# Turning the gate weights by transposing transfers in place of TensorE, and the b2 product two slots later

## What is computed

```python
def attention(ctx, x, Wq):                       # causal, 64 tokens a sequence
    q = x @ Wq.T; k = v = ctx @ Wq.T
    return softmax(mask(q @ k.T / sqrt(128))) @ v

def ffn(x, gate_W, W1, b1, W2, b2):
    gates = softmax(x @ gate_W)                  # 8 experts
    cw = the two largest gates of a token, normed to 1, zero elsewhere
    out = x
    for e in range(8):
        h = relu(x @ W1[e] + b1[e])              # 128 -> 256
        out = out + cw[:, e:e+1] * (h @ W2[e] + b2[e])
    return out

x = x + attention(ctx, layernorm(x), Wq)
x = x + ffn(layernorm(x), gate_W, W1, b1, W2, b2)
```

## Time and profile before

| | |
|---|---|
| time, median of 3 runs | 131.17 us (130.90 to 131.28) |
| the profiled execution, its time | 130.83 us |
| the profiled execution, its span | 129.0 us |
| TensorE busy in the span | 120.3 us (93%), 1175 products |
| VectorE busy | 107.6 us (83%) |
| ScalarE busy | 93.5 us (73%) |
| GpSimd busy | 53.5 us (41%) |
| granted TensorE clock | full in all 40 slices |

### The profile page before, as it was taken

How to read it: one execution, slowest core, us unless ns; L and a number is a source line. 1 busy time by engine, 2 the same in 40 slices (tenths; PEclk the granted TensorE clock), 3 DMA queues, 4 the chain that set the end, 5 groups by cost and what they waited for, 6 DMA issues and landing times. The chain is left out here.

```text
span 129.0 us, 3295 instructions
## 1 busy us (share of the span) xinstructions
PE 120.3 (93%) x1175; PEld 90.7 (70%) x1175; DVE 107.6 (83%) x419; ACT 93.5 (73%) x191; POOL 53.5 (41%) x57
## 2 busy tenths in 40 slices
PE   6987788999979999999999999999999979999991
PEld 2585566777847768778768778778776757776690
DVE  0629998989999999989898999958998798866683
ACT  3337485999776955996779927993799467989830
POOL 7199155330094951330095640330468303345400
PEclk9999999999999999999999999999999999999999
DMA  3999900000000000200000000200000002000002
GB/s 92 321 283 321 289 26 8 0 0 0 5 0 0 0 5 3 81 0 5 0 0 5 0 3 13 68 5 0 3 0 8 0 0 86 3 0 0 5 0 81
DMA packets 9904, 5.54 MB, mean 43 GB/s; under 512 B 504, under 2 KB 9888, under 8 KB 9888
## 3 DMA queue, kind: packets, MB, share of 16 engines
q1 hardware_dynamic: 9744, 5.27, 15.2%
q10 hardware_dynamic: 144, 0.07, 0.2%
HBM read 4.28 MB, written 1.05 MB: 41 GB/s over the span
## 5 line engine op out<-in xcount | busy, mean ns | idle before, releaser
L690 POOL TENSOR_TENSOR h_lo<-h,h_hi 128x512 f16<-128x512 f32 x24 | 28.7, 1196 | 40.2 <-ACT h L571 39.9
L571 ACT ACTIVATE h<-psH,b1T 128x512 f32<-128x512 f32 x64 | 43.3, 689 | 1.1 <-PE psH L508 0.9
L570 ACT ACTIVATE h_hi<-psH,b1T 128x512 f16<-128x512 f32 x48 | 33.0, 688 | 11.5 <-PE psH L387 11.4
L864 DVE SCALAR_TENSOR_TENSOR acc<-psY,weight_y,acc 128x128 f32<-128x128 f32 x125 | 35.1, 342 | 1.4 <-PE psY L408 1.2
L383 PE MATMUL psH<-x_hi,w_hi 128*128 128x512 f16 x62 | 23.5, 379 | 1.0 <-ACT h L571 1.0
L387 PE MATMUL psH<-x_lo,w_hi 128*128 128x512 f16 x62 | 23.5, 379 | 0.0
L384 PE MATMUL psH<-x_hi,w_lo 128*128 128x512 f16 x62 | 23.5, 379 | 0.0
L848 DVE TENSOR_TENSOR h_lo<-h,h_hi 128x512 f16<-128x512 f32 x24 | 16.5, 689 | 7.8 <-ACT h L571 7.3
L408 PE MATMUL psY<-w_hi,h_hi 128*128 128x128 f16 x192 | 22.7, 219 | 0.0
L408 PE MATMUL psY<-w_lo,h_hi 128*128 128x128 f16 x192 | 22.7, 219 | 0.0
L408 PEld LDWEIGHTS psY<-w_hi,h_hi 128*128 128x128 f16 x192 | 15.3, 98 | 2.2
(11 more groups left out here) (191 smaller groups left out, 191.4 us busy)
## 6 DMA issues: line engine op xcount, KB each, us to landing
w_sb<-in_L_ffn_W_dram SPq DMA_DIRECT2D x8, 256.0 KB, 4.9
out_dram<-acc SPq DMA_DIRECT2D x3, 256.0 KB, 2.3
x_sb<-in_x_dram SPq DMA_DIRECT2D x2, 256.0 KB, 4.0
ctx_sb<-in_ctx_dram SPq DMA_DIRECT2D x2, 256.0 KB, 4.4
x_sb<-in_x_dram SPq DMA_DIRECT2D x1, 512.0 KB, 7.6
ctx_sb<-in_ctx_dram SPq DMA_DIRECT2D x1, 512.0 KB, 8.5
out_dram<-acc SPq DMA_DIRECT2D x2, 128.0 KB, 1.8
wq_sb<-in_L_xattn_Wq_dram ACTq DMA_DIRECT2D x1, 64.0 KB, 2.8
```

What stands on the lines that cost most here:

```text
L570: nc.scalar.activation(h_hi[:, C * (e % 2) + c, :], psH[c][:, :], ACT.Relu, bias=bias, scale=scale)
L571: nc.scalar.activation(h[:, C * (e % 2) + c, :], psH[c][:, :], ACT.Relu, bias=bias, scale=scale).then_inc(h_ready, 1)
L690: nc.gpsimd.tensor_tensor(h_lo[:, i, :], h[:, i, :], h_hi[:, i, :], ALU.subtract).then_inc(hlo0_ready, 1)
L864: last = nc.vector.scalar_tensor_tensor(out=o, in0=y, scalar=weight_y[:, g % 2, t, e:e + 1], in1=o, op0=ALU.mult, op1=ALU.add)
```

## The change

weight_cat becomes 128 columns a tile wide and weight_catT 128 partitions high. The 16-bit identity, its memset and its select on GpSimd go. TensorE's transposes at slot 3 and ScalarE's copy go. SP issues, for each group, four transposing transfers from SBUF to SBUF (`turn_cat`), one a tile, as soon as cat_ready and, from group 1 on, the b2 product of the group before allow it. The b2 product goes from slot 4 to slot 6 and waits for the four transfers; the addition on VectorE goes from slot 5 to slot 7. VectorE waits for the transfers of the group before ahead of writing weight_cat.

```diff
-        ident16 = sb("ident16", [P, P], fp16)
...
-        weight_cat = sb("weight_cat", [P, TG, NB2], fp16)
-        weight_catT = sb("weight_catT", [NB2, TG, P], fp16)
+        weight_cat = sb("weight_cat", [P, TG, P], fp16)
+        weight_catT = sb("weight_catT", [P, TG, P], fp16)
...
-        CAT_T, B2_PRODUCT, B2_ADD = 3, 4, 5
+        B2_PRODUCT, B2_ADD = 6, 7
...
+            def turn_cat(g):
+                sp.wait_ge(cat_ready, g + 1)
+                if g > 0:
+                    sp.wait_ge(b2_ps, g)
+                for t in range(TG):
+                    sp.dma_start_transpose(weight_catT[:, t, :], weight_cat[:, t, :]).then_inc(cat_turned, 16)
+
+            turn_cat(0)
             for g in range(0, GROUPS - 1):
+                turn_cat(g + 1)
                 store(g)
...
-            def cat_transposes(g):
-                pe.wait_ge(cat_ready, g + 1)
+            def b2_product(g):
+                pe.wait_ge(cat_turned, (g + 1) * TG * 16)
                 for t in range(TG):
-                    last = nc.tensor.transpose(cat_ps[:, t, :], weight_cat[:, t, :], ident16[:, :])
-                last.then_inc(catT_ps, 1)
-
-            def b2_product(g):
-                pe.wait_ge(catT_ready, g + 1)
-                for t in range(TG):
-                    last = nc.tensor.matmul(tiles(psD)[:, t, :], weight_catT[:, t, :], b2_cat[:, :],
+                    last = nc.tensor.matmul(tiles(psD)[:, t, :], weight_catT[0:NB2, t, :], b2_cat[:, :],
                                             start=True, stop=True)
                 last.then_inc(b2_ps, 1)
...
-            group_steps = {CAT_T: cat_transposes, B2_PRODUCT: b2_product}
...
-                if slot in group_steps:
-                    group_steps[slot](g)
+                if slot == B2_PRODUCT:
+                    b2_product(g)
...
-            def cat_out(g):
-                act.wait_ge(catT_ps, g + 1)
-                copy(weight_catT[:, :, :], cat_ps, catT_ready)
...
-                if slot == CAT_T:
-                    cat_out(g)
...
-            nc.gpsimd.memset(ident16[:, :], 0.0).then_inc(const_zero, 1)
...
-            nc.gpsimd.affine_select(out=ident16[:, :], in_=ident16[:, :], compare_op=ALU.not_equal, fill=1.0,
-                                    base=0, pattern=[[-1, P]], channel_multiplier=1).then_inc(const_zero, 1)
...
                 if a >= 1:
-                    dve.wait_ge(catT_ps, a)
+                    dve.wait_ge(cat_turned, a * TG * 16)
```

More of the change, by code:

```diff
@@ L206, in xattn_moe @@
         logits_ps, below_ready, gate_exp_ready = sem("logits_ps"), sem("below_ready"), sem("gate_exp_ready")
-        cat_ready, catT_ps, catT_ready, b2_ps, b2_added = (
-            sem("cat_ready"), sem("catT_ps"), sem("catT_ready"), sem("b2_ps"), sem("b2_added"))
+        cat_ready, cat_turned, b2_ps, b2_added = sem("cat_ready"), sem("cat_turned"), sem("b2_ps"), sem("b2_added")
         z_ps, h_ready, hlo0_ready, hlo_ready = sem("z_ps"), sem("h_ready"), sem("hlo0_ready"), sem("hlo_ready")
@@ L357, in logit_product @@
                 last.then_inc(logits_ps, 1)
-            cat_ps = psD[0:NB2, 0:TG * P // 2].bitcast(fp16).rearrange("p (t n) -> p t n", n=P)
-            def cat_transposes(g):
-                pe.wait_ge(cat_ready, g + 1)
+            def b2_product(g):
+                pe.wait_ge(cat_turned, (g + 1) * TG * 16)
                 for t in range(TG):
-                    last = nc.tensor.transpose(cat_ps[:, t, :], weight_cat[:, t, :], ident16[:, :])
-                last.then_inc(catT_ps, 1)
-            def b2_product(g):
-                pe.wait_ge(catT_ready, g + 1)
-                for t in range(TG):
-                    last = nc.tensor.matmul(tiles(psD)[:, t, :], weight_catT[:, t, :], b2_cat[:, :],
+                    last = nc.tensor.matmul(tiles(psD)[:, t, :], weight_catT[0:NB2, t, :], b2_cat[:, :],
                                             start=True, stop=True)
@@ L648, in _ @@
             nc.gpsimd.memset(ident[:, :], 0.0).then_inc(const_zero, 1)
-            nc.gpsimd.memset(ident16[:, :], 0.0).then_inc(const_zero, 1)
             nc.gpsimd.memset(mask[:, :], 0.0).then_inc(const_zero, 1)
-            pool.wait_ge(const_zero, 3)
+            pool.wait_ge(const_zero, 2)
             nc.gpsimd.affine_select(out=ident[:, :], in_=ident[:, :], compare_op=ALU.not_equal, fill=1.0, base=0,
                                     pattern=[[-1, P]], channel_multiplier=1).then_inc(const_ready, 1)
-            nc.gpsimd.affine_select(out=ident16[:, :], in_=ident16[:, :], compare_op=ALU.not_equal, fill=1.0,
-                                    base=0, pattern=[[-1, P]], channel_multiplier=1).then_inc(const_zero, 1)
             nc.gpsimd.affine_select(out=mask[:, :], in_=mask[:, :], compare_op=ALU.is_ge, fill=MASKED, base=0,
                                     pattern=[[-1, P]], channel_multiplier=1).then_inc(const_zero, 1)
+            pool.wait_ge(const_zero, 3)
+            nc.gpsimd.memset(mask[SEQ:P, 0:SEQ], MASKED).then_inc(const_zero, 1)
+            pool.wait_ge(const_zero, 4)
+            nc.gpsimd.memset(restart[:, :, :], 1.0).then_inc(const_zero, 1)
             pool.wait_ge(const_zero, 5)
[L660 to L663, removed]
             nc.gpsimd.memset(restart[:, :, 0:1], 0.0)
```

## The result

| | kernel before | changed kernel |
|---|---|---|
| median | 131.03 us (130.89 to 131.28, 4 runs) | 134.51 us (133.95 to 135.15, 4 runs) |
| ratio, 95% interval | | 1.0258 [1.0211, 1.0306] |
| profiled execution | 130.83 us, span 129.0 | 134.98 us, span 133.2 |

The change costs 2.6%, about 3.5 us. The time lies inside the stated range (130.3 to 138), but it is not the forecast of 131.2: the range reached so far only because of rival 2, and rival 2 came. Beside it VectorE made TensorE wait in group 0, as forecast, but by another mechanism and for longer.

What follows compares the result with a forecast made beforehand. TensorE was taken as the bound. Group 0's +0.75 us and groups 1 to 3's -0.69 gave +0.06 on the profiled 130.83, so 130.9; with the median 0.34 higher, 131.2 us, range 130.3 to 138.

Steps and rivals of the forecast that it cites:

- rival 2: At TensorE's b2 product: transfers outlast their window, from 0.95 us an issue; 133.0 us at 1.2, up to 160; chance 0.41.
- TensorE is the bound, and its waits for other engines decide: Between 20 and 125 us TensorE is busy 102.8 of 105.0 us; removed work shortens the run except ahead of its waits.
- 0.23 us of transposes per group: Four TensorE transposes at slot 3 go, 0.92 us over four groups; groups 1 to 3 keep 0.23 us each.
- TensorE's other waits lie elsewhere: ScalarE's four dropped copies, 2.4 us, were costed at nothing because TensorE's remaining waits for ScalarE were not there.
- Transfers at 0.6 to 0.9 us an issue: On SP's queue a group's four transfers take 4.2 to 5.4 us, hidden in windows of 5.6 to 6.6 us.
- Group 0: The moved addition makes VectorE about 0.75 us late; TensorE's gate product waits for x_lo, +0.75 us against before.
- The power should have been passed over: In group 0 GpSimd's power gets in only at 36.7, ends at 37.7, and TensorE goes on at about 39.0.
- rival 1: In group 0 the power gets in between w_lo and h_lo, VectorE loses 0.2 us at most: 130.7 us; chance 0.26.
- The other groups on VectorE: In groups 1 to 3 VectorE has idle time behind ScalarE, so the moved addition of 0.72 us fits in.
- SP, the stores, ScalarE's copies, GpSimd's start: Stores queued behind transfers, four dropped copies and GpSimd's changed start were all costed at nothing.
- The sum: For the run, +0.75 us in group 0 and -0.69 in groups 1 to 3 make +0.06 us, forecast 131.2 us.
- its case: The forecast's likeliest case, transfers hidden and group 0 late on VectorE: 130.9 to 131.6 us, chance 0.33.

Runs made afterwards that it cites:

- no_turn_45: Changed kernel with transfers and turning left out, b2 product on unturned weights, product and addition at slots 4 and 5: 131.06 us, ratio 0.9981.
- packed_pe: Kernel before with a group's weights packed into one 128 x 128 block, one TensorE transpose and a 128-column copy per group: 131.89 us, ratio 1.0012.
- idle_turns: Kernel before plus sixteen transposing transfers between two spare buffers, for which no engine waits until the last store: 131.74 us, ratio 1.0006.
- move_only: Kernel before, TensorE transposes kept, with the b2 product moved to slot 6 and its addition to slot 7: 132.94 us, ratio 1.0111.
- add_only: Kernel before with only the b2 addition moved, from slot 5 to slot 7: 132.32 us, ratio 1.0065.
- turn_later: Changed kernel with the b2 product at slot 8 and its addition at slot 9: 132.72 us, ratio 1.0105.
- turn_6_10: Changed kernel with the b2 product kept at slot 6, addition at slot 10, gate product also waiting for the addition: 133.49 us, ratio 1.0117.

## Where the prediction was right, and where it was wrong

- **TensorE is the bound, and its waits for other engines decide**: right. All of the loss behind the head is waits of TensorE.
- **0.23 us of transposes per group**: the price is right (-0.23 at expert 3 in each group). That groups 1 to 3 keep it is wrong, and so is the claim that TensorE's other waits lie elsewhere. no_turn_45 ends 0.17 us ahead of the kernel before in the profiled executions, 0.29 with its later head taken off, where 0.69 was credited to groups 1 to 3 alone. The step looked at idle time of TensorE's matmuls; the wait for h stood in its weight loads, 0.27 us at 58.12, three products behind the saved transposes.
- **Transfers at 0.6 to 0.9 us an issue**: wrong, 1.23 us. It was the term that carried most: the margin was given correctly (it decides from 0.95 us an issue), and the choice near the lower end had only the remark behind it that 32 KB is small. Rival 2 at 1.2 us an issue said 0.4, 0.4 and 1.0 us in groups 1 to 3, 133.0 us; measured some 0.3, 0.6 and 1.6. The prediction added four issues and a landing, though the landing (2.4 us) counts from the start of the last issue: in group 0, with no long issue, the four took 6.15 us and not 6.6. The one long issue in each of the other groups, which the rival did not have, took that back and more. Rival 2 was right in kind and place.
- **Group 0**: right that TensorE waits for a late x_lo, wrong in how it comes about. The gate product slipped by 1.50 us (45.91 against 44.41), 1.17 without the head, where +0.75 was forecast; with the addition alone moved it is 1.26, of which the head has 0.09. Two steps failed. The power should have been passed over and xf should have ended as before, so that all 0.72 us of the addition come on top. But the power took 1.32 us, not 1.9, TensorE went on at 38.69, not 39.0, and the addition made VectorE only 0.14 us late at w_lo, as rival 1 had it up to this point (0.2 us at most). Then the keep-out struck where nobody had looked: w_lo had gone from 0.30 us ahead of GpSimd's h_lo to 0.18 us behind it, and lost 0.97 us. That the forecast of a loss of this kind came true in group 0 is therefore partly luck.
- **The other groups on VectorE**: right that the 0.72 us fits in. Behind the addition VectorE still stood idle for h, 0.35 us ahead of 69.51 and 0.84 ahead of 72.08. The 0.52 us of group 1 came of something else: h_lo and GpSimd's sum start within 0.01 us of each other, GpSimd came first, h_lo took 1.83 us, and TensorE waited 0.34 us for x_lo at 74.57. packed_pe has this wait with the addition at its old place, so it is not put down to the change.
- **SP, the stores, ScalarE's copies, GpSimd's start**: costed at nothing, and nothing is seen of them. The three stores behind the transfers take 0.58 us to issue in place of 0.37 to 0.39, and nobody waits for them; idle_turns bears out that the traffic is free.
- **The sum.** The forecast of 131.2 us was 3.3 us too low, and its case and rival 2 were treated as exclusive. They can come together: the move without transfers measured 1.1% and 0.7% (move_only, add_only), the addition out of the way 1.2% with the waits for transfers left, both 2.6%. Two causes with a chance each should have been added, not divided among cases. That 134.5 us still lies in the range is due to the width given to rival 2, whose own 133.0 us lacks the part of VectorE.

## What to carry to other kernels

When an instruction moves on an engine that keeps another out and is kept out by it, write down the start times of both engines' instructions for the whole stretch up to the next point where TensorE waits, shift the one row, and look at who comes first in each pair: here coming 0.2 us behind cost 1 us. Work saved on TensorE counts only up to the next wait of its weight loads, so read that row before crediting it. Small transfers in a row on one queue cost their number times the issue: pack them into one before you move on-chip work to them, and compare that with doing nothing.

## What the runs showed that was not expected

- A two-operand instruction of GpSimd of 1.28 us makes a VectorE instruction with two SBUF operands that starts up to 0.18 us behind it 1.65 to 1.83 us long in place of 0.69 (w_lo at 41.50 and 41.26, h_lo at 72.08 and 99.43). The b2 addition, with one operand in PSUM, was not held: 0.69 us at 98.71 in turn_later, under GpSimd's h_lo of 98.20 to 99.36. Two SBUF operands are not the only case: the second xf of the changed kernel, with one tensor operand in SBUF, took 1.20 us from 38.55 on in place of 0.34, under GpSimd's h_lo of 38.51.
- The order of h_lo and GpSimd's sum is a tie that flips with 0.01 us. In group 1 of the kernel before VectorE's h_lo came first, in the trace of the changed kernel the sum of GpSimd did; in group 2 of the changed kernel h_lo came first again (101.01 against 101.02) and took 0.69 us. It may be part of why executions of one kernel differ by over 1 us, but that was not tried. Timelines of both engines, the kernel before, then the changed one:

```profile
70.36 0.69 DVE L848 TENSOR_TENSOR h_lo<-h,h_hi 128x512 f16<-128x512 f32 x1 [0.37 <-ACT h L571]
...
70.37 1.82 POOL L682 TENSOR_TENSOR acc<-x,xf 128x512 f32<-128x512 f32 x1
```

```profile
72.08 1.83 DVE L835 TENSOR_TENSOR h_lo<-h,h_hi 128x512 f16<-128x512 f32 x1 [0.84 <-ACT h L564]
...
72.08 1.29 POOL L669 TENSOR_TENSOR acc<-x,xf 128x512 f32<-128x512 f32 x1
```

- A 128 x 128 two-byte transposing transfer from SBUF to SBUF takes 1.1 to 1.23 us of its queue, in groups 1 to 3 once 1.7 to 2.4 us. Why one in a group is longer was not tried.
- In the trace of turn_6_10 the granted clock fell behind a single wait of TensorE of 1.9 us, at 103.52: it is 1.00 from 104 to 105 us, 0.51 from 105 to 106, 0.50 to 108. In the changed kernel, whose longest wait is 1.41 us, it stays at 1.00.
